# A third of the second lot's upper payload words moves from VectorE to GpSimd in a row sort

## What is computed

```python
idx = jnp.argsort(vf, axis=-1)
vs = jnp.take_along_axis(vf, idx, axis=-1)
gat = lambda t: jnp.take_along_axis(t.reshape(b, c, hw), idx, axis=-1)
out1 = _reshape_attn(gat(q1), gat(k1), vs, temperature, True)
out2 = _reshape_attn(gat(q2), gat(k2), vs, temperature, False)
inv = jnp.argsort(idx, axis=-1)
out1 = jnp.take_along_axis(out1, inv, axis=-1).reshape(b, c, h, w)
```

## Time and profile before

| | us |
|---|---|
| median of 3 runs (15140.57 to 15142.44) | 15142.0 |
| the profiled execution | 15131.19 |
| its span | 15129.3 |
| VectorE busy in the span | 13763.9 (91%) |
| ScalarE busy | 7104.4 (47%) |
| TensorE matmuls | 6739.8 (45%) |
| GpSimd busy | 6003.8 (40%) |

### The profile page before, as it was taken

One profiled execution on the slowest core, in us unless ns is written; L12 is line 12 of the kernel. 1 busy time (PEld: TensorE's weight loads), 2 busy tenths in 40 slices (PEclk: granted clock), 3 DMA queues, 4 the chain that ended last, 5 costly groups with the idle time before them and its releaser, 6 DMA issues. The chain is left out here.

```text
span 15129.3 us, 121619 instructions
## 1 busy us (share of the span) xinstructions
PE 6739.8 (45%) x42188; PEld 2753.7 (18%) x42188; DVE 13763.9 (91%) x8241; ACT 7104.4 (47%) x6587; POOL 6003.8 (40%) x4372
## 2 busy tenths in 40 slices
PE   4777744481025625714814723833732015433310
PEld 2443421120012211211201211211211002111100
DVE  4777778899999999999999999999999999989978
ACT  0000003355575565565565566566566555444443
POOL 0000000066666666666666666666666640000000
PEclk8888877795557857856956966966866557666655
DMA  1554553110001000100100100100100001221232
GB/s 33 123 134 109 131 118 76 55 43 13 12 12 35 27 12 30 32 12 30 31 12 26 36 12 23 38 12 12 45 17 12 33 29 53 84 66 54 77 76 66
DMA packets 343162, 699.24 MB, mean 46 GB/s; under 512 B 71581, under 2 KB 275582, under 8 KB 331702
## 3 DMA queue, kind: packets, MB, share of 16 engines
q1 hardware_dynamic: 342518, 691.17, 17.1%
HBM read 480.98 MB, written 209.95 MB: 46 GB/s over the span
## 5 line engine op out<-in xcount | busy, mean ns | idle before, releaser
L1183 DVE COPY_PREDICATED arena<-psum,arena 128x4096 f32<-128x4096 uint32 (+26 forms) x1456 | 4009.6, 2771 | 46.4 <-ACT psum L1143 45.8
L1190 DVE COPY_PREDICATED arena<-psum,arena 128x4096 f32<-128x4096 uint32 (+26 forms) x1456 | 3969.2, 2742 | 42.0
L1009 PE MATMUL psum<-arena,wt 128*32 128x448 f32 x31360 | 3224.9, 573 | 1239.5 <-DMA arena<-xpad 698.8
L1108 POOL TENSOR_TENSOR arena<-arena 128x1024 int32<-128x1024 int32 (+26 forms) x1456 | 2077.7, 1433 | 3061.6 <-DVE arena L1175 3058.2
L1094 POOL TENSOR_TENSOR arena<-arena 128x1024 bf16<-128x1024 f32 (+26 forms) x1456 | 1975.6, 1363 | 3284.0 <-SPq L267 3081.3
L1131 ACT ACTIVATE arena<-arena 128x4096 f32<-128x4096 f32 (+26 forms) x1456 | 3071.7, 2126 | 71.1 <-DVE arena L1190 38.0
L1151 ACT ACTIVATE masks<-psum 128x512 fp8e4<-128x512 f32 (+27 forms) x1256 | 923.6, 736 | 3563.6 <-DVE arena L1190 3562.5
L1100 POOL TENSOR_TENSOR arena<-arena 128x1024 int32<-128x1024 int32 (+26 forms) x1456 | 2006.1, 1384 | 0.0
L1009 PEld LDWEIGHTS psum<-arena,wt 128*32 128x32 f32 x31360 | 1039.5, 115 | 3427.5 <-issue 2326.4
L1399 PE MATMUL psum<-ident,arena 128*112 128x128 f32 x896 | 197.1, 386 | 2443.1 <-ACT arena L1318 1879.8
L1175 DVE TENSOR_TENSOR arena<-arena 128x1024 f32<-128x1024 f32 (+26 forms) x1456 | 1163.4, 812 | 100.4 <-POOL arena L1100 100.4
(11 more groups left out here) (131 smaller groups left out, 7837.8 us busy)
## 6 DMA issues: line engine op xcount, KB each, us to landing
arena<-xpad SPq DMA_DIRECT2D x896, 108.5 KB, 2.3
arena<-simd SPq DMA_DIRECT2D x416, 210.0 KB, 4.3
arena<-simd SPq DMA_DIRECT2D x416, 196.0 KB, 4.4
xpad<-arena SPq DMA_DIRECT2D x8, 1924.0 KB, 14.6
arena<-in_x SPq DMA_DIRECT2D x8, 1568.0 KB, 7.3
x3d<-arena SPq DMA_DIRECT2D x8, 1568.0 KB, 5.3
prodd<-arena SPq DMA_DIRECT2D x8, 1568.0 KB, 5.1
arena<-prodd SPq DMA_DIRECT2D x8, 1568.0 KB, 14.0
```

The source lines that it names most:

```text
L1009: last = nc.tensor.matmul(psum[C * b:C * b + C, n % C_BANKS, 0:CROWS * W], wt[:, g, C * w:C * w + C], cx[i % 2][b][:, y0:y0 + CROWS, x0:x0 ...
L1108: last = nc.gpsimd.tensor_tensor(hi, packed_view(stmp, here, piece, 1), lo, ALU.subtract)
L1183: last = nc.vector.copy_predicated(lo, wide_mask(q, k, piece, here), hi)
L1190: last = nc.vector.copy_predicated(hi, wide_mask(q, k, piece, here), packed_view(ptmp, here, piece, NP))
```

## The change

The first lot of each step stays as it is. In the second lot, `shared_lot` splits the pairs into kept and given ones, the given ones being the last 32% or so (`POOL_SHARE = (0, 0.32)`), cut at borders that leave the pieces regular. Over a round 12,768 of the 40,420 pairs are given, in 106 pieces; the kept ones have 92 pieces, where the whole second lots had 103.

VectorE's lower copy still covers the whole lot. ScalarE saves low words, and VectorE copies upper words, only for the kept pairs. For the given ones GpSimd writes lo + hi of all four payload words, as integers, into their place in `ptmp` before the lower copy (`pay_sums`), and sum - lo to the upper words after it (`pay_uppers`). New semaphores: `k_ps` (sums done; the lower copy of lot 1 waits for it) and `k_pu` (uppers done; `keep_pay` of lot 1 and the next `pay_sums` wait for it). GpSimd's order is written anew: for each step uppers of lot 0, differences and sums of the next step's lot 0, the same three for lot 1, then `pay_uppers`, then `pay_sums` of the next step. Before the step LAST_LEVEL the differences and sums come behind `pay_uppers`.

```diff
--- before.py
+++ after.py
@@ -177,7 +177,62 @@
 
 LOT_TMP = max(lot_at(q, 1) + lot_size(q, 1) for q in range(len(ROW_LOTS)))
 assert all(lot_size(q, 0) <= lot_at(q, 1) for q in range(len(ROW_LOTS)))
+POOL_SHARE = (0, 0.32)
+
+
+def cut_piece(piece, x, slack):
+
+
+    base, nb, sb, j0, ng, sg, w, d = piece
+    block, n = ng * w, size(piece)
+    for unit in (block, w, 8, 1):
+        if w % unit and unit < w:
+            continue
+        c = min(n, max(0, round(x / unit) * unit))
+        if abs(c - x) <= slack:
+            break
...
+    assert sum(map(size, low)) == c and sum(map(size, low + high)) == n
+    return low, high
+
+
+def shared_lot(rows, share):
+
+
+    total = sum(size(piece) for piece, _ in rows)
+    x, slack = total * (1 - share), total / 16
+    kept, given = [], []
+    for piece, _ in rows:
+        low, high = cut_piece(piece, min(size(piece), max(0, x)), slack)
+        kept += low
+        given += high
+        x -= size(piece)
+    return kept, given
+
+
+SHARED = [[shared_lot(rows, share) for rows, share in zip(lots, POOL_SHARE)] for lots in ROW_LOTS]
 for q, (first, second) in enumerate(ROW_LOTS):
+    assert SHARED[q][0][0] and not SHARED[q][0][1] and all(SHARED[q][1])
     assert sum(size(x) for x, _ in first + second) == ROW_NET[q][2]
     assert not touched(first) & touched(second)
     if q and q != LAST_LEVEL:
@@ -1030,10 +1085,11 @@
 
 
         k_df, k_sm, k_up = ([sem(f"k_{n}{k}") for k in range(2)] for n in ("df", "sm", "up"))
+        k_ps, k_pu = sem("k_ps"), sem("k_pu")
         d_mw, d_mcp, d_cp, d_lo, d_hi = ([sem(f"d_{n}{k}") for k in range(2)] for n in ("mw", "mcp", "cp", "lo", "hi"))
         d_lv = [sem(f"d_lv{k}") for k in range(2)]
         d_mst = [sem(f"d_mst{i}") for i in range(4)]
-        d_sems = [*k_df, *k_sm, *k_up, *d_mw, *d_mcp, *d_cp, *d_lo, *d_hi, *d_lv, *d_mst]
+        d_sems = [*k_df, *k_sm, *k_up, k_ps, k_pu, *d_mw, *d_mcp, *d_cp, *d_lo, *d_hi, *d_lv, *d_mst]
         pmask = psum[:, 4:8, :].rearrange("p k n -> p (k n)")
 
         def lot_rows(q, k):
@@ -1041,6 +1097,14 @@
             here = lot_at(q, k)
             for piece, at in ROW_LOTS[q][k]:
                 yield piece, at, here
+                here += size(piece)
+
+        def shared_rows(q, k, part):
+
+            kept, given = SHARED[q][k]
+            here = lot_at(q, k) + (sum(map(size, kept)) if part else 0)
+            for piece in (kept, given)[part]:
+                yield piece, here
                 here += size(piece)
 
         def word_at(q, k):
@@ -1108,17 +1172,43 @@
                     last = nc.gpsimd.tensor_tensor(hi, packed_view(stmp, here, piece, 1), lo, ALU.subtract)
                 last.then_inc(k_up[k], 1)
 
+            def pay_sums(q):
+                if q:
+                    pool.wait_ge(d_hi[0], q)
+                    pool.wait_ge(d_hi[1], q)
+                    pool.wait_ge(k_pu, q)
+                for piece, here in shared_rows(q, 1, 1):
+                    lo, hi = pair_views(pay[b].bitcast(i32), piece, NP)
+                    last = nc.gpsimd.tensor_tensor(packed_view(ptmp.bitcast(i32), here, piece, NP), lo, hi, ALU.add)
+                last.then_inc(k_ps, 1)
+
+            def pay_uppers(q):
+                pool.wait_ge(k_ps, q + 1)
+                pool.wait_ge(d_lo[1], q + 1)
+                for piece, here in shared_rows(q, 1, 1):
+                    lo, hi = pair_views(pay[b].bitcast(i32), piece, NP)
+                    last = nc.gpsimd.tensor_tensor(hi, packed_view(ptmp.bitcast(i32), here, piece, NP), lo, ALU.subtract)
+                last.then_inc(k_pu, 1)
+
+            def prepare(q, k):
+                differ(q, k)
+                sums(q, k)
+
+            prepare(0, 0)
+            prepare(0, 1)
+            pay_sums(0)
             for q in range(SR):
-                if q == LAST_LEVEL:
-                    uppers(q - 1, 1)
-                differ(q, 0)
-                sums(q, 0)
-                if q and q != LAST_LEVEL:
-                    uppers(q - 1, 1)
-                differ(q, 1)
-                sums(q, 1)
-                uppers(q, 0)
-            uppers(SR - 1, 1)
+                ahead = q + 1 < SR and q + 1 != LAST_LEVEL
+                for k in range(2):
+                    uppers(q, k)
+                    if ahead:
+                        prepare(q + 1, k)
+                pay_uppers(q)
+                if q + 1 == LAST_LEVEL:
+                    prepare(q + 1, 0)
+                    prepare(q + 1, 1)
+                if q + 1 < SR:
+                    pay_sums(q + 1)
 
         def d_scalar(act, b, beside, slots=SLOTS):
 
@@ -1127,7 +1217,8 @@
                     act.wait_ge(d_hi[k], q)
                     if k or q == LAST_LEVEL:
                         act.wait_ge(d_hi[1 - k], q)
-                for piece, _, here in lot_rows(q, k):
+                        act.wait_ge(k_pu, q)
+                for piece, here in shared_rows(q, k, 0):
                     last = nc.scalar.activation(packed_view(ptmp, here, piece, NP), pair_views(pay[b], piece, NP)[0],
                                                 ACT.Copy)
                 last.then_inc(d_cp[k], 1)
@@ -1177,6 +1268,8 @@
 
             def lower(q, k):
                 dve.wait_ge(d_cp[k], q + 1)
+                if k:
+                    dve.wait_ge(k_ps, q + 1)
                 dve.wait_ge(d_mw[k], q + 1)
                 for piece, _, here in lot_rows(q, k):
                     lo, hi = pair_views(pay[b], piece, NP)
```

More of the change, by code:

```diff
@@ L179, with group @@
 assert all(lot_size(q, 0) <= lot_at(q, 1) for q in range(len(ROW_LOTS)))
+POOL_SHARE = (0, 0.32)
[8 more added lines that the diff above has]
+            break
+    b, rest = divmod(c, block)
+    g, i = divmod(rest, w)
+    low, high = [], []
+    def group(into, lo, hi):
+        if lo < hi:
+            into.append((base + b * sb, 1, sb, j0 + g * sg + lo, 1, 0, hi - lo, d))
+    if b:
+        low.append((base, b, sb, j0, ng, sg, w, d))
+    if g:
+        low.append((base + b * sb, 1, sb, j0, g, sg, w, d))
+    group(low, 0, i)
+    if i:
+        group(high, i, w)
+    first = g + (i > 0)
+    if rest and first < ng:
+        high.append((base + b * sb, 1, sb, j0 + first * sg, ng - first, sg, w, d))
+    done = b + (rest > 0)
+    if done < nb:
+        high.append((base + done * sb, nb - done, sb, j0, ng, sg, w, d))
+    assert sum(map(size, low)) == c and sum(map(size, low + high)) == n
[11 more added lines that the diff above has]
+SHARED = [[shared_lot(rows, share) for rows, share in zip(lots, POOL_SHARE)] for lots in ROW_LOTS]
 for q, (first, second) in enumerate(ROW_LOTS):
+    assert SHARED[q][0][0] and not SHARED[q][0][1] and all(SHARED[q][1])
     assert sum(size(x) for x, _ in first + second) == ROW_NET[q][2]
```

## The result

The changed kernel takes 15428.95 us (15422.13 to 15434.44, 4 runs) against 15142.22 us: ratio 1.019 (95% interval 1.0174 to 1.0207), so 287 us slower. The forecast was slower, 15,580 us, with the range 15,090 to 15,900.

The account below looks back on a forecast made before the run. VectorE's instruction stream was taken to bound the sort. Per round +61 us, eight rounds 488, less some 40, gave +450; with 15131 and 11 that is 15592, stated as 15,580 us, range 15,090 to 15,900.

Parts of the forecast that it names:

- the exclusion: In the sort, a GpSimd operation and VectorE's two-input value minimum do not overlap; a minimum takes 2.10 against 1.19 us.
- the wait at step 66: At step LAST_LEVEL, VectorE idles 2.8 us a round because GpSimd must finish pay_uppers before the differences.
- What VectorE loses: Words and instructions taken off VectorE's upper copies in the second lots: 60 us per round, 480 us in all.
- What GpSimd gains: Payload sums and subtractions added to GpSimd: 261 us per round, 2090 us in all.
- The walk of a near-full step: Step of 1016/539 pairs: 0.75 us saved, 1.4 or so lost in waits, so 16.4 to 16.8 against 15.92 us.
- the 512 step: Step of 512/256 pairs, 8.58 us before: GpSimd needs 10.8 us, part of its lag carried on, so +1.4 us each.
- the relief from the attention's operations: Where VectorE does the attention's small operations GpSimd catches up: some 40 us off the eight rounds' 488.
- The last level: Steps of 512/1024-1055 pairs: 18.7 us against 15.94, less lag carried, +14 us a round for its 8 steps.
- The rival of the plain bound: GpSimd's own work bounds the kernel: payload operations at 2.5 ns an element, +129 us per round, 16,160 us; chance 0.08.
- Edits at no cost: ScalarE's extra wait before keep_pay of lot 1 and VectorE's wait for pay_sums cost nothing, except in the last level.
- the work hides: Rival: GpSimd's 261 us fit into its 382 us of waits per round; about 14,760 us, chance 0.15.
- The draw: Rival: waits of 0.6 to 0.9 us per step leave the time at 15,112 to 15,172 us; chance 0.07.

Follow-up runs that it names:

- the pair of masked kernels: Value minimum replaced by a predicated copy with its mask in PSUM, ScalarE making mask words first: changed kernel 15183.14 us, kernel before 15422.07 us.
- the memset run: Changed kernel with every GpSimd payload operation replaced by a memset of as many words, which writes SBUF and reads nothing: 14805.87 us, ratio 0.9776.
- without payload work: Changed kernel with pay_sums and pay_uppers each cut to a one-column memset, same waits and semaphores: 14768.91 us, ratio 0.9754.
- the changed kernel with the predicated copy: Changed kernel, value minimum replaced by a predicated copy with its mask in PSUM, ScalarE making mask words before saving payload: 15183.14 us, ratio 1.0025.
- the small share: Changed kernel with GpSimd given 10% of the second lot in place of 32% from step 69 on: 15267.32 us, ratio 1.0079.
- half the share: Changed kernel with GpSimd's share of the second lot at 0.16 in place of 0.32 everywhere: 15097.85 us, ratio 0.9974.

## Why the prediction was right, and where its sizes were off

*What bounds the kernel, and the exclusion.* Right: the pair of masked kernels and the attention's two multiplications show it, and the single meetings in the memset run have the same 2.10 us as the earlier trace rows.

*The size as a whole.* The forecast put the cost of all waiting at 450 + 480 = 930 us, 22 of them for the wait at step 66. Measured are 287 + 456 = 743: 660 for the payload work and 82 for the order. The first was put too high and the second too low, and that they partly cancel is luck.

*What VectorE loses.* 480 us forecast, 444 measured in L1283 and 456 without payload work. The price of a word, 1.14 ns, was right to 5%.

*What GpSimd gains.* 2090 us forecast, 2045 measured where nothing holds it up, 2395 beside the minima.

*The walk of a near-full step.* Forecast 16.4 to 16.8 us, measured 16.83 in the one shown; in the 15 such steps up to step 54 of the first round the mean went from 15.90 to 16.35, +0.45, where the sum took +0.6. The walk put a wait of 1.2 us at the second minimum or of 1.6 at the first. The one shown has 1.5 at the second. The walk counted 685 words given away in the step of 1016/539 pairs, which gives 632.

*The other kinds of step.* This is where most of the 150 us between 15,580 and 15,429 came from. First round, from the starts of the minima in the timeline:

| pairs in lot 0 | steps | forecast, us | measured, us |
|---|---|---|---|
| 1024 | 10 | -7 | -1.8 |
| 512 | 9 | +12.6 | +2.4 |
| 768 | 8 | +7.6 | +6.2 |
| 896 | 7 | +4.9 | +2.7 |
| 960 | 6 | +2.4 | +2.2 |
| 992 to 1022 | 15 | +9 | +6.8 |
| steps 55 to 69 | 15 | +16 | +9.8 |
| last level, lot 1 of step 70 to that of 77 | 7 | +14 (of 8) | +18.0 |
| sum | | 60 | 46.3 |

The term that was mis-sized most is the 512 step: +1.4 us each, measured +0.27. Its sum of 10.8 us was about right as work: in the changed kernel with the predicated copy, where nothing holds GpSimd up, its operations take 10.0 us on average in the eight such steps before one of 768 pairs, and the two minima 1.2. But the steps last 9.4 us on average, so most of the lag must be carried into the steps around, and I had let only a part be carried. The 1024 step beside it was charged too little (-0.7 each, measured -0.2), which gives back half of that error. The second is the relief from the attention's operations: the seven rounds that have them lost (287 - 46)/7 = 34 us each on average, so 12 less than the first, where I had taken off 5 a round. That the relief comes from these operations was not tested.

*The last level.* +14 us a round forecast, +18 measured, 162 us back from the small share. The walk said that the cover for `pay_sums` would be gone in the last level only, and so it is: there are 60 waits of VectorE for it, up to 3.0 us long. What the sum treated as exclusion alone is for about two fifths GpSimd's own amount of work, as the run with the predicated copy shows. The rival of the plain bound is thus shown for these steps and for no others.

*The signs.* L1190 by -450: it was -444. L1175 by 1000 us or more, to over 2000: this was not met, it grew by 514 to 1677. The whole cost was 743 and not 930, and 168 of it are waits in front of L1276, 35 the attention's multiplication. GpSimd's busy time past 8000 us: 8466. Its waits for minima well under 1500: 809. The lower copies unchanged: yes.

*Edits at no cost.* ScalarE's longer wait in front of `keep_pay` cost nothing in the changed kernel, where VectorE waits for no saved words; in the masked kernels it does cost, up to 225 us. GpSimd's new order was put at nothing outside of step 66, and is 82 us without payload work: mainly 54 in longer minima, 23 in waits for mask words and 14 at step 66. Step 66 was put at 2.8 us a round; it is 3.1 in the changed kernel and 1.7 without payload work. Why the order lengthens the minima and the waits for mask words was not tested.

*The rivals.* That the work hides was given 0.15, with waits under 0.75 us a step as its condition. At half the share it comes true, if barely: 0.26% faster. Its price was summed wrongly: a quarter of the forecast's own 930 us is 232 and not 100, so that it should have read about 14,890. The draw's 0.6 to 0.9 us a step is too wide as well: over 78 steps and 8 rounds 0.15 us is 94 us, and the band given was 30 us to either side.

## What to carry to other kernels

Moving work to an idle engine is worth what the idle time covers, but look where that idle time lies: here GpSimd's pauses stood in front of VectorE's two-input operations and kept them free, so that filling them cost VectorE more than the work that it was relieved of. Look in the timeline for an operation that is longer when the other engine is busy than when it is idle, price the change by the sum of the two engines' times that exclude each other, and take a small share first: half the share had a quarter of the lengthening. Here the exclusion went when the operation was written with one of its inputs in PSUM, and the same move then gained 239 us, but the new form cost 280 us by itself until it was kept to the steps where it is as cheap, and the whole won 1.1% only with the smaller share in the narrow steps and in the last level.

## What the runs showed of the hardware that was not expected

A predicated copy of single words in strides of two (1023 pairs, width 1) takes 2508 ns against 1217 of the minimum, while at 1024 pairs it averages 1467 ns over all widths, and a pair costs 1.2 to 1.5 ns from width 4 on. The payload copies with four words an element don't show this: 1.1 to 1.25 ns a word.

Minima that start inside a memset of GpSimd last 12 ns (median) longer than free ones, those that start inside a reading operation 291 ns (179 and 375 cases of the memset run).

Not every operation with a single SBUF input is free of GpSimd: a `tensor_scalar` with eight columns a partition (L1450, 16 times in the changed kernel) takes 1153 to 1261 ns in the 7 cases where it starts inside a sum of GpSimd, and 145 to 173 ns in the other 9. It costs 7 us in all, and no run asks why it differs from the copies.
